# Attention on one Trainium2 core: the vector engine's additions split around its second maxima, and RoPE's sine products made by GpSimd

## The reference

```python
h = (x - mu) * rsqrt(var + LN_EPS) * ln_scale + ln_bias
q = ((h @ w_down_q.T) @ w_up_q.T)      # k the same way, v = c_kv @ w_up_v.T
q, k = rope(q), rope(k)                # rot = x * cos + swapped(x) * sin
scores = einsum('bhqd,bhkd->bhqk', q, k) / sqrt(64)
out = einsum('bhqk,bhkd->bhqd', softmax(scores), v)
out = out @ w_out.T + residual
```

## Time and profile before

| | |
|---|---|
| median of 3 runs | 3764.19 us (3763.82 to 3764.31) |
| the profiled execution's own time | 3764.86 us |
| its span, first to last instruction | 3763.3 us |
| mean granted TensorE clock | 0.995 of full speed |
| TensorE busy over the span | 3674.8 us (98%) |
| DVE busy | 3210.0 us (85%) |
| ScalarE busy | 2778.0 us (74%) |
| GpSimd busy | 1236.9 us (33%) |

### The profile page before, as it was taken

The page is one execution under the profiler, slowest core; times in us unless marked ns, Lnnn a source line. Parts: engine busy times, 40 slices in busy tenths (PEclk is TensorE's granted clock), DMA queues, the critical chain, the costliest instruction groups (busy, mean ns, idle before and its releaser), DMA issues. The chain is left out here.

```text
span 3763.3 us, 76388 instructions
## 1 busy us (share of the span) xinstructions
PE 3674.8 (98%) x23848; PEld 2361.9 (63%) x23848; DVE 3210.0 (85%) x4340; ACT 2778.0 (74%) x4016; POOL 1236.9 (33%) x1178
## 2 busy tenths in 40 slices
PE   7989999999999999999999999999999999999999
PEld 5754444444444444444444444444499999999999
DVE  8868888888888888888888888888777777777799
ACT  5767878777877878787787778787766666666665
POOL 2202232222222222222222222323266666666500
PEclk9999999999999999999999999999999999999999
DMA  7975666666666666666666666666466666666798
GB/s 269 355 245 135 168 167 164 166 170 159 169 162 160 172 159 163 170 165 160 169 163 162 170 157 166 167 164 147 144 228 215 217 216 214 221 219 222 231 362 275
DMA packets 378435, 724.72 MB, mean 193 GB/s; under 512 B 105277, under 2 KB 253886, under 8 KB 342272
## 3 DMA queue, kind: packets, MB, share of 16 engines
q0 software_dynamic: 83504, 340.66, 34.5%
q1 hardware_dynamic: 292816, 382.71, 31.2%
q10 hardware_dynamic: 2048, 0.53, 0.1%
HBM read 453.60 MB, written 138.81 MB: 157 GB/s over the span
## 5 line engine op out<-in xcount | busy, mean ns | idle before, releaser
L1160 ACT ACTIVATE at_ex<-at_st 128x1024 f32<-128x1024 f32 x1024 | 1047.2, 1023 | 111.1 <-PE at_st L1325 97.9
L1338 PE MATMUL at_pv<-at_ex,at_v 128*64 128x512 f32 x4096 | 993.2, 606 | 0.0
L1019 DVE TENSOR_REDUCE at_mx<-at_fr 128x1 f32<-128x512 f32 x1024 | 700.9, 684 | 287.1 <-PE at_fr L1345 192.9
L1184 ACT ACTIVATE at_fr<-at_fr 128x512 f32<-128x512 f32 x1024 | 599.9, 586 | 360.8 <-PE at_fr L1348 310.1
L1032 DVE TENSOR_TENSOR at_sum<-at_sum,at_ex 128x1024 f32<-128x1024 f32 x448 | 546.7, 1220 | 12.4 <-ACT at_ex L1160 2.9
L1338 PEld LDWEIGHTS at_pv<-at_ex,at_v 128*64 128x64 f32 x4096 | 248.6, 136 | 479.3 <-issue 463.9
L1348 PE MATMUL at_fr<-at_kfar,at_qh 64*128 64x512 f32 x1024 | 469.4, 458 | 34.2 <-DVE at_mx L1019 21.0
L1345 PE MATMUL at_fr<-at_kdif,at_qh 64*128 64x512 f32 x1024 | 475.4, 464 | 3.5 <-DVEq L674 2.5
L1345 PEld LDWEIGHTS at_fr<-at_kdif,at_qh 64*128 64x128 f32 x1024 | 188.0, 184 | 417.2 <-issue 412.9
L1860 PE MATMUL ex_o<-ex_w,ex_hT 128*128 128x256 f32 x3408 | 426.0, 285 | 0.9 <-DVE ex_out L1725 0.9
L1844 PE MATMUL ex_h<-ex_xT,ex_w 128*128 128x256 f32 x3408 | 422.4, 284 | 1.8 <-DVE ex_w L1678 1.8
(11 more groups left out here) (208 smaller groups left out, 6171.9 us busy)
## 6 DMA issues: line engine op xcount, KB each, us to landing
at_cq<-scr_c SPq DMA_DIRECT2D x62, 1024.0 KB, 5.9
at_ck<-scr_c SPq DMA_DIRECT2D x62, 1024.0 KB, 5.0
at_sum<-at_sum POOLq DMA_DIRECT2D x95, 512.0 KB, 5.5
scr_v<-pj_v SPq DMA_DIRECT2D x64, 512.0 KB, 6.9
at_v<-scr_v SPq DMA_DIRECT2D x64, 512.0 KB, 8.0
mid_rec<-scr_rec SPq DMA_DIRECT2D x256, 128.0 KB
scr_o<-mid_oT SPq DMA_DIRECT2D x64, 512.0 KB
at_rotq<-at_swpq POOLq DMA_DIRECT2D x126, 256.0 KB, 4.5
```

What stands on the lines that cost most here:

```text
L1019: e.reduce_max(mx[k // QB][:, h * QB + k % QB:h * QB + k % QB + 1], fr[h][:, :], AX.X).then_inc(s_tr[h], 1)
L1160: e.activation(ex[k][:, :, :], st[u % 2][:, :, :], ACT.Exp, scale=SCALE).then_inc(s_exp, 1)
L1184: e.activation(fr[h][:, :], fr[h][:, :], ACT.Relu).then_inc(s_pos[h], 1)
L1338: mm = e.matmul(pv[n][rows[h], :], v[i.u][:, kt, rows[h]], ex[kt][:, h, :], start=(kt == 0), stop=(kt == KT - 1))
```

## The change

In every body of the attention:

- `turn_sin` moves from DVE to GpSimd, where it stands right ahead of the `add_swapped` of the same operand. It waits for the projected rows (`s_raw`) there. The same holds for the second pair's two products in the prologue, for which GpSimd now also waits for the tables.
- In an even step, where two additions fall due, the first goes ahead of the second maximum and the other stays behind it. In an odd step the one addition stays behind.
- `normalise(.., 0)` moves from ahead of the second maximum of g = 2 to the end of g = 4, `normalise(.., 1)` from ahead of that of g = 6 to the end of g = 7, and `recip` from the end of g = 6 to g = 7.

```diff
@@ gpsimd
+            def turn_sin(j, x):
+                rotated(e, j.next(-1), x)
+                wait_apart(e, s_raw[x], j.n(2, 2), s_apart)
+                e.tensor_tensor(out=swp[x][:, :], in0=raw[x][:, :], in1=sin[:, :], op=ALU.mult).then_inc(s_prod[x], 1)
...
                 if ahead >= 2:
+                    turn_sin(i.next(2), Q)
                     add_swapped(i.next(2), Q)
                 if ahead:
                     add_sums(i, 0)
                 if ahead >= 2:
+                    turn_sin(i.next(2), K)
                     add_swapped(i.next(2), K)
@@ vector
-            def turn_sin(j, x):
...
+            def additions(i, prev, g):
+                j, u = (i, 2 * g - 2) if g else (prev, UNITS - 2)
+                due = [(j, u // KT, m) for m in (u % KT, u % KT + 1) if j and m % (KT // 2)]
+                return (due[:-1], due[-1:])
...
-                    if g == 2 and older:
-                        normalise(prev.next(-1), 0)
...
-                    if g == 6 and older:
-                        normalise(prev.next(-1), 1)
                     if g == 7 and more:
                         low(one, K)
+                    early, late = additions(i, prev, g)
+                    for added in early:
+                        add_keys(*added)
                     if g < 2 or more:
                         maximum(*slot_of(i, g), 0, s_y)
-                    if g:
-                        add_two(i, 2 * g - 2)
-                    elif prev:
-                        add_two(prev, UNITS - 2)
+                    for added in late:
+                        add_keys(*added)
                     if g == 1 and more:
                         low(one, Q)
-                    if g == 3 and most:
-                        turn_sin(two, Q)
-                    if g == 5 and most:
-                        turn_sin(two, K)
-                    if g == 6 and prev:
+                    if g == 4 and older:
+                        normalise(prev.next(-1), 0)
+                    if g == 7 and prev:
                         recip(prev)
+                    if g == 7 and older:
+                        normalise(prev.next(-1), 1)
```

More of the change, by code:

```diff
@@ L958, in prologue @@
                 e.wait_ge(s_made, 5)
+                e.wait_ge(s_const, 48)
                 for x in (Q, K):
+                    turn_sin(At(0, 1), x)
                     add_swapped(At(0, 1), x)
@@ L982, in turn_cos @@
                 e.tensor_tensor(out=rot[x][:, :], in0=raw[x][:, :], in1=cos[:, :], op=ALU.mult).then_inc(s_prod[x], 1)
-            def turn_sin(j, x):
-                rotated(e, j.next(-1), x)
-                e.tensor_tensor(out=swp[x][:, :], in0=raw[x][:, :], in1=sin[:, :], op=ALU.mult).then_inc(s_prod[x], 1)
             def first_turn(x):
@@ L1072, in prologue @@
                         turn_cos(second, Q)
-                    if k == 2:
-                        turn_sin(second, Q)
                     if k == 3:
@@ L1083, in prologue @@
                         low(first, K)
-                    if k == 3:
-                        turn_sin(second, K)
                     if k == 4:
@@ L1135, in tail @@
             def tail(i):
-                add_two(i, UNITS - 2)
+                for n, k in ((1, KT - 2), (1, KT - 1)):
+                    add_keys(i, n, k)
                 for n in range(NH2):
```

## The result

The changed kernel takes **3836.21 us** (median of 4 runs, 3835.19 to 3837.29), against 3764.25 for the kernel before beside it: 1.019 times as long, with a 95% interval of 1.0172 to 1.0208. It is 72 us slower. The forecast was 3746 and the range 3687 to 3805, so the result lies outside it, on the side of rival C.

A forecast was written before the change was run, and what follows sets the result against it. TensorE was taken to bound the kernel, with 1.27 us of pause per 38.42 us pair. Reordering gave 37.25, GpSimd's hold added 0.86: 38.11, saving 18.6 us over 60 pairs, so 3746 us; range 3687 to 3805.

The forecast's parts named there:

- rival C: GpSimd's products hold DVE too long, in step 1's addition and `low` and step 5's cosine product: 3792 to 3828; chance 0.25.
- What bounds the kernel, and the additions: TensorE sets the pace; 1.27 us of each pair is pause in steps 1, 3 and 7, which reordering DVE's additions removes.
- the walk: DVE's new order timed through unpaused steps from step 0's `step_x`: no pause from DVE; with step 1's remainder, 37.25 us a pair.
- case A: DVE isn't held, or hardly, by GpSimd's products: 1.17 us a pair go, 70 us, giving 3694; chance 0.30.
- rival D: ScalarE's ReLU takes over the pauses in steps 3 and 7: some 0.2 us a pair stay, 12 us; only widens other cases.
- What stays in step 1: ScalarE's late ReLU lets `step_y` start at 1.82 instead of 1.72 us after `step_x`: 0.10 us a pair left.
- The hold itself: A GpSimd product reading all the time holds DVE's two-input work for its whole length, from where both want to read.
- D: Length of one 128x1024 GpSimd sine product: taken as 2.1 us, between bounds of 1.1 and 2.8.
- The place: The queries' product starts behind step 1's key steps and holds the addition, pausing step 2 by D - 1.24 = 0.86 us.
- the formula: For the queries' product behind the key steps: a pause of D - 1.24 us in step 2, 0.86 at 2.1.
- The keys' product: It holds the cosine product ahead of step 5's second maximum: a pause of D - 2.13 us, none at 2.1.
- Moved finishing work: `normalise` and `recip` stand in DVE gaps of 0.9 and 0.6 us, already counted: costs nothing.

The follow-up runs named there:

- the order alone: The changed kernel's new order with both sine products put back on DVE, behind the late additions of steps 3 and 5: 3693.47 us.
- the kernel with the fill: The changed kernel with GpSimd's sine products replaced by a memset of the same 128x1024 tile: 3718.41 us, a single run.
- the copy: The changed kernel with GpSimd's sine products replaced by a one-input copy of the projected rows, without the sine multiplication: 3739.82 us, a single run.

## Why the prediction failed

*What bounds the kernel, and the additions: right.* The pair with the products left on DVE takes 37.29 us for the 37.25 of the walk, and the time is 3693 for the 3694 of case A. In the order alone steps 3 and 7 last 4.81 us, and their `step_y` comes 1.72 behind `step_x`, so the pauses there were DVE's alone and rival D is out.

*What stays in step 1: 0.10 foreseen.* `step_y` starts 1.74 us behind `step_x`, only 0.02 later than in an unpaused step, but the step as a whole lasts 4.92 us for 4.80. The size was right, the place not quite.

*The hold itself: right, though only assumed.* "I take it that a GpSimd product which reads all the time holds DVE's two-input work for D" is what the runs show: one to one with the length, by reads and not by writes. The Trainium skill ("SBUF — State Buffer", Who interferes with whom) says so, and these traces agree with 3.78 us for 0.95 and 2.89 for 1.22. Rival A, at a chance of 0.30, is out. The subtraction within the power was weak evidence for it: that power reads 8 elements, and the kernel with the fill shows that writing alone doesn't hold such an instruction.

*The place: the step that failed.* The queries' product "is ready at 6.25 and starts at 6.67, behind the key steps": ready it was, but it didn't go behind them. The prediction took it that a DVE instruction already started keeps its right. In the walk's time, from the `step_x` of step 0 at 1563.04, the subtraction starts at 5.71, and the product is recorded from 5.95 to 8.67. A lead of 0.24 us was too little for DVE, so the subtraction is held until 9.49, and the second maximum of step 1 with it. The product itself ends no later than forecast (8.67, for 6.67 + 2.1 = 8.77). What costs is that the subtraction and a maximum now stand behind it, ahead of the addition and `low`. That adds a pause ahead of `step_x`, the very sign that the prediction named for being wrong altogether. Steps 1 and 2 lost 2.22 us a pair where 0.86 had been foreseen: 1.36 us more, about 82 us over 60 pairs. With the keys' 7 that makes 89 of the 90 us by which the measured time is above the forecast.

*D: mis-sized, but that is not what failed.* The forecast took 2.1. It is 2.37 by itself, and 2.72 as recorded behind a DMA issue. The price of one input was right: the copy takes 1.04 us after a wait, where the earlier trace rows had given 1.1. The second input costs 1.33 us (2.37 less 1.04), and not 0.88. At the place foreseen, 2.37 would have made the pauses 1.13 and 0.24 instead of 0.86 and none, 31 us in all, so 3777, inside the stated range. With the product behind the key steps the formula holds once the start is put where it was (1.56 us for the 1.54 measured).

*The keys' product: none foreseen, 0.12 us a pair measured,* in step 6 of the changed kernel. D - 2.13 would give 0.24 at 2.37. It costs more, 0.60, only in the kernel where the queries' product has been moved into step 4 and pushes it 0.5 us later. So the price of one hold depends on where the other one lies.

*Moved finishing work: nothing foreseen, 11 us measured,* by a wait in step 0 that the walk of DVE didn't contain.

*Rival C* had the hold and gave 3828 at 2.8, but that it comes so near to 3836 is luck. It placed the cost in the addition and `low` of step 1 and in the cosine product, not in the subtraction, and at the product's own 2.37 us its formula, 37.25 + 2D - 3.37, gives 38.62 us a pair, 3776. What spoke against it was only that 2.8 would be three streams one behind the other, while the prediction itself held a slower routine to be likelier than a faster one. Between bounds of 1.1 and 2.8 a value had been chosen by a picture of ports; a decision point at 2.27, so near to the chosen 2.1, should have carried more of the chance.

## What to carry to other kernels

Before work goes to GpSimd, find which DVE instruction will stand beside it and what stands behind that one: a GpSimd instruction that reads SBUF and goes first holds a DVE instruction with two inputs until it ends. Here two such products a pair, 2.7 us each by their records, cost 143 us in all, while the same products ahead of DVE's slack cost 3. Start such work by a wait at the beginning of a known gap, and don't cut it up.

And where one engine's order of jobs makes another pause, try the order alone first: it brought 71 us with no work moved.

## What the runs showed of the hardware that was not expected

- Of two records that overlap, the earlier isn't always the one that goes first: with a lead of 0.24 us a DVE subtraction was held by GpSimd's product (3.78 us), a cosine product with 0.33 to 0.35 too (4.13), and a subtraction with 0.43 or more wasn't (0.95). GpSimd's product was then hardly longer than before (2.75). One addition with a lead of 0.17 wasn't held either.
- A waiting DVE instruction gets no turn between GpSimd instructions that follow one another directly: four of 256 columns took 3.13 us, and DVE's was held for 4.20.
- GpSimd's writes alone leave DVE's instructions with two inputs at their pace (0.946 us) but hold DVE's plain fp32 copy, from 0.28 to 1.87 us, in 22 of 48 cases.
- An instruction of GpSimd recorded directly behind a DMA issue starts before that issue's record ends, and is longer by about as much: the product 2.72 against 2.37 us, the copy 1.39 against 1.04, the overlap 0.32 to 0.35.
